# A DLRM tower on one Trainium2 core: first chunk tile by tile, a sum over d in four pieces, late columns' passes ahead of layer 1's last sum

## What is computed

```python
e  = stack([tbl_f[ids[:, f]] for f in range(39)], axis=1)        # 512 x 39 x 16 (b, field, d)
z0 = einsum('bid,bjd->bdij', e, e)                               # all pairs, per d
cur0 = relu(einsum('bdk,kl->bld', z0.reshape(b, d, 39*39), W0))  # 128 features
next_h, direct0 = split(cur0, 2, axis=1)                         # 64 + 64
z1 = einsum('bid,bjd->bdij', e, next_h)
cur1 = relu(einsum('bdk,kl->bld', z1.reshape(b, d, 39*64), W1))  # 128 features
z  = sum(concatenate([direct0, cur1], axis=1), axis=-1)          # the sum over d: 512 x 192
h  = relu(concatenate([z, dense_ctx], axis=1) @ W_top1 + b_top1) # 512 x 512
y  = relu(h @ W_top2 + b_top2) @ W_top3                          # 512 x 1
```

## Time and profile before

| | us |
|---|---|
| median of three runs | 447.23 |
| the three runs | 426.04, 447.23, 447.35 |
| the profiled execution | 425.06 |
| its span, first to last instruction | 423.2 |
| PE / DVE / POOL / ACT busy in the span | 393.7 / 347.0 / 284.4 / 226.8 |

### The profile page before, as it was taken

How to read it: one execution, slowest core, us unless ns; L and a number is a source line. 1 busy time by engine, 2 the same in 40 slices (tenths; PEclk the granted TensorE clock), 3 DMA queues, 4 the chain that set the end, 5 groups by cost and what they waited for, 6 DMA issues and landing times.

```text
span 423.2 us, 4060 instructions
## 1 busy us (share of the span) xinstructions
PE 393.7 (93%) x1417; PEld 248.8 (59%) x1417; DVE 347.0 (82%) x198; ACT 226.8 (54%) x225; POOL 284.4 (67%) x164
## 2 busy tenths in 40 slices
PE   0695999999899979999899999999999999999997
PEld 0452656565666646564665656566656565666655
DVE  1205879979999799897989999999999999999930
ACT  1333466474656466473648475665747474655422
POOL 5777878989888889898888888888888600000000
PEclk9899899999999989999899999999999999999999
DMA  7194969596978979694978969797969395997000
GB/s 285 29 207 98 284 170 222 167 227 152 268 172 217 209 191 219 172 266 107 251 180 217 232 203 233 192 250 191 265 171 284 108 283 184 269 259 199 1 2 0
DMA packets 27862, 80.80 MB, mean 191 GB/s; under 512 B 7265, under 2 KB 16225, under 8 KB 20034
## 3 DMA queue, kind: packets, MB, share of 16 engines
q1 hardware_dynamic: 22354, 78.43, 71.0%
q0 software_dynamic: 5120, 1.32, 2.9%
q10 hardware_dynamic: 368, 0.80, 0.5%
HBM read 76.58 MB, written 3.93 MB: 190 GB/s over the span
## 4 chain that ended last, share of the span: by engine, by line
PE 51%; POOL 36%; issue 7%; DMA 5%; ACT 0%; DVE 0%; SPq 0%
POOL found L285 36%; PE acc L517 10%; PE acc L543 8%; PE acc L544 8%; PE acc L551 8%; PE acc L562 6%; PE sums L500 4%; DMA found<-in_table_dram,rows_sb 3%; PE acc L558 2%; PE spread L591 2%; DMA x_parts<-x_rows 1%; PE spread L530 1%; DMA x_rows<-found 1%; PE sums L580 0%; PE sums L582 0%
## 5 line engine op out<-in xcount | busy, mean ns | idle before, releaser
L285 POOL DMA_INDIRECT found<-in_table_dram,rows_sb x160 | 284.2, 1776 | 51.2 <-issue 48.5
L428 DVE TENSOR_TENSOR z_lo<-z,z_hi 128x2048 fp32r<-128x2048 f32 x64 | 146.1, 2284 | 8.6 <-ACT z_hi L328 8.4
L328 ACT ACTIVATE z_hi<-z 128x2048 fp32r<-128x2048 f32 x63 | 120.4, 1912 | 57.7 <-DVE z L420 57.7
L420 DVE TENSOR_TENSOR z<-x_wide,h 128x2048 f32<-128x2048 f32 x64 | 145.4, 2285 | 6.8 <-DMA x_wide<-x_rows 6.4
L543 PE MATMUL acc<-z_hi,w_hi 128*128 128x512 f32 x256 | 108.8, 425 | 0.0
L517 PE MATMUL acc<-squares,w 128*128 128x512 f32 (+1 forms) x224 | 108.0, 599 | 0.0
L544 PE MATMUL acc<-z_hi,w_lo 128*128 128x512 f32 x256 | 102.3, 399 | 0.0
L304 ACT ACTIVATE squares<-sums 128x1024 f32<-128x1024 f32 x64 | 58.5, 913 | 61.3 <-PE sums L500 61.3
L551 PE MATMUL acc<-z_lo,w_hi 128*128 128x512 f32 x256 | 82.2, 443 | 0.0
L551 PEld LDWEIGHTS acc<-z_lo,w_hi 128*128 128x128 f32 x256 | 48.2, 188 | 23.1 <-issue 15.4
L543 PEld LDWEIGHTS acc<-z_hi,w_hi 128*128 128x128 f32 x256 | 49.5, 193 | 14.8 <-issue 4.2
(11 more groups left out here) (49 smaller groups left out, 135.0 us busy)
## 6 DMA issues: line engine op xcount, KB each, us to landing
x_wide<-x_rows SPq DMA_DIRECT2D x64, 512.0 KB, 7.6
x_wide<-x_rows SPq DMA_DIRECT2D x112, 256.0 KB, 9.5
x_parts<-x_rows SPq DMA_DIRECT2D x31, 128.0 KB, 2.5
x_rows<-found SPq DMA_DIRECT2D x16, 240.0 KB, 2.6
x_wide<-x_rows SPq DMA_DIRECT2D x16, 192.0 KB, 7.2
found<-in_table_dram,rows_sb POOLq DMA_INDIRECT x160, 7.0
w_sb<-in_w_dram SPq DMA_DIRECT2D x1, 1280.0 KB, 8.4
x_wide<-x_rows SPq DMA_DIRECT2D x16, 64.0 KB, 6.7
```

Source lines behind the costliest of these rows:

```text
L285: pool.indirect_dma_start(out=found[:, b, 2, s * D:s * D + D], out_offset=None, in_=table, in_offset=bass.IndirectOffsetOnAxis(ap=rows_sb[ ...
L328: nc.scalar.activation(z_hi[:, n % RING], z[:, n % RING], ACT.Copy).then_inc(hi_done, 1)
L420: nc.vector.tensor_tensor(z[:, n % RING], x, h[:, c % 2, :].unsqueeze(1).to_broadcast([P, QUADS, N]), ALU.mult).then_inc(multiplied, 1)
L428: nc.vector.tensor_tensor(z_lo[:, n % RING], z[:, n % RING], z_hi[:, n % RING], ALU.subtract).then_inc(lo_done, 1)
```

## The change

- Chunk 0's layer 0 goes by single tiles (`add_up_tile`, `square_tile`, `contract0_tile`) with semaphores counted in tiles; later chunks keep groups of two.
- At the start DVE does `split(0)` ahead of the addition of W0's halves; PE does 17 dummy products at once and 9 behind the small `mix` product, and no longer waits for the first split.
- PE does `contract1_hi(0)` ahead of chunk 1's first `add_up`, and `contract1_lo(0)` ahead of the second.
- ACT's `split(2)` stands at n = 0 in place of g = 1; DVE's `reduce0(1)` stands at n = 4 in place of n = 6.
- `reduce1` is four instructions of 8 samples each in place of one of 32.
- After the last `contract1_lo`, PE does the products of `feat_b` for the late columns at once, then half of `y_of(early)`, and after `reduce1` only the products of `feat_a`; the other half of `y_of(early)` stands behind them.

```diff
+def tiles0(q):
+    return q // ND * T0 + q % ND * 2
@@ SP, and likewise evict0 and hid1_of
-                    sp.wait_ge(summed, ND * (c - BUFS + 1))
+                    sp.wait_ge(summed, T0 * (c - BUFS + 1))
@@ ACT
+            def square_tile(t):
+                rows = slice(0, P) if t < T0 - 1 else slice(HALF, P)
+                act.wait_ge(summed, t + 1)
+                if t >= 2 * RING0:
+                    act.wait_ge(contracted0, t - 2 * RING0 + 1)
+                nc.scalar.activation(squares[rows, t // 2 % RING0, t % 2, :], sums[rows, t % 2, :],
+                                     ACT.Square).then_inc(squared, 1)
...
-            for d in range(ND):
-                square(d)
+            for t in range(T0):
+                square_tile(t)
             split(1)
             evict0(0)
...
                     if g < 2 and c + 1 < CHUNKS:
                         square(ND * (c + 1) + 2 + g)
+                    if n == 0:
+                        split(2)
...
-                    if g == 1 and c + 2 < CHUNKS:
+                    if g == 1 and 0 < c < CHUNKS - 2:
                         split(c + 2)
@@ DVE
             def reduce1(c):
                 dve.wait_ge(evicted1, c + 1)
-                nc.vector.tensor_reduce(feat_a[:, c * CB:c * CB + CB],
-                                        cur1[:, :].rearrange("p (b d) -> p b d", d=D), AX.X,
-                                        ALU.add).then_inc(reduced1, 1)
+                for i in range(0, CB, CB // 4):
+                    last = nc.vector.tensor_reduce(feat_a[:, c * CB + i:c * CB + i + CB // 4],
+                                                   cur1[:, i * D:(i + CB // 4) * D].rearrange("p (b d) -> p b d", d=D),
+                                                   AX.X, ALU.add)
+                last.then_inc(reduced1, 1)
...
+            split(0)
             dve.wait_ge(w0_in, 32)
...
-            split(0)
             dve.wait_ge(w1_hi_ready, 1)
...
+                    if n == G - 1:
+                        reduce0(1)
                     if is_v(n):
                         low_part(n)
...
-                    if n == G + 1:
-                        reduce0(1)
@@ PE
+            def add_up_tile(t):
+                if t == 0:
+                    pe.wait_ge(placed[0], 32)
+                if t >= 2:
+                    pe.wait_ge(squared, t - 1)
+                nc.tensor.matmul(sums[:, t % 2, :], select_sb[:, t, :], x_parts[:, 0, :],
+                                 start=True, stop=True).then_inc(summed, 1)
...
+                if batch == late:
+                    return
                 nc.tensor.matmul(hid1_acc[m][:, batch], wt1a_sb[:, cols], feat_a[:, batch],
                                  start=False, stop=True).then_inc(hid1_done, 1)
+
+            def hid1_end(m):
+                nc.tensor.matmul(hid1_acc[m][:, late], wt1a_sb[:, m * P:m * P + P], feat_a[:, late],
                                  start=False, stop=True).then_inc(hid1_done, 1)
...
             pe.wait_ge(select_ready, 1)
+            keep_busy(acc0, 17)
             pe.wait_ge(w0_ready, 1)
...
-            pe.wait_ge(found_hi_done, 1)
-            keep_busy(acc0, 21)
-            add_up(0)
+            keep_busy(acc0, 9)
+            add_up_tile(0)
+            add_up_tile(1)
             spread_out(0)
             pe.wait_ge(w0_ready, 2)
-            for d in range(ND):
-                if d + 1 < ND:
-                    add_up(d + 1)
-                contract0(d)
+            for t in range(T0):
+                if t + 2 < T0:
+                    add_up_tile(t + 2)
+                contract0_tile(t)
             keep_busy(acc1, 14)
...
+            contract1_hi(0)
             add_up(ND)
-            contract1_hi(0)
+            contract1_lo(0)
             add_up(ND + 1)
             contract0(ND)
-            contract1_lo(0)
...
             contract1_lo(G * CHUNKS - 1)
-            y_of(early)
             pe.wait_ge(reduced0, CHUNKS)
+            pe.wait_ge(hid1_relu, M1 // P)
+            for m in range(M1 // P):
+                hid1_of(m, late)
+            y_of(0, early)
             pe.wait_ge(reduced1, CHUNKS)
             for m in range(M1 // P):
-                hid1_of(m, late)
+                hid1_end(m)
+            y_of(1, early)
```

More of the change, by code:

```diff
@@ L501, in add_up, with contract0_tile @@
                                             start=True, stop=True)
-                last.then_inc(summed, 1)
+                last.then_inc(summed, len(DUOS[q % ND]))
+            def add_up_tile(t):
[5 more added lines that the diff above has]
+                                 start=True, stop=True).then_inc(summed, 1)
+            def contract0_tile(t):
+                pe.wait_ge(squared, t + 1)
+                rows = slice(0, P) if t < T0 - 1 else slice(HALF, P)
+                nc.tensor.matmul(acc0[:, :], w0[rows, t, :], squares[rows, t // 2 % RING0, t % 2, :],
+                                 start=(t == 0), stop=(t == T0 - 1)).then_inc(contracted0, 1)
             def keep_busy(acc, count):
@@ L518, in contract0 @@
                                             start=(t == 0), stop=(t == T0 - 1))
-                last.then_inc(contracted0, 1)
+                last.then_inc(contracted0, len(DUOS[d]))
             def spread_out(n):
@@ L593, in hid2_of, with y_of @@
                 last.then_inc(hid2_done, 1)
-            def y_of(batch):
-                for k in range(M2 // P):
-                    pe.wait_ge(hid2_relu, k + 1 + (M2 // P if batch == late else 0))
-                    last = nc.tensor.matmul(y_acc[:, batch], wt3_sb[:, k:k + 1], hid2[k][:, batch],
-                                            start=(k == 0), stop=(k == M2 // P - 1))
-                last.then_inc(y_done, 1)
+            def y_of(k, batch):
+                pe.wait_ge(hid2_relu, k + 1 + (M2 // P if batch == late else 0))
+                last = nc.tensor.matmul(y_acc[:, batch], wt3_sb[:, k:k + 1], hid2[k][:, batch],
+                                        start=(k == 0), stop=(k == M2 // P - 1))
+                if k == M2 // P - 1:
+                    last.then_inc(y_done, 1)
             pe.wait_ge(select_ready, 1)
+            keep_busy(acc0, 17)
             pe.wait_ge(w0_ready, 1)
@@ L670, in _ @@
             contract1_lo(G * CHUNKS - 1)
-            y_of(early)
             pe.wait_ge(reduced0, CHUNKS)
+            pe.wait_ge(hid1_relu, M1 // P)
+            for m in range(M1 // P):
+                hid1_of(m, late)
+            y_of(0, early)
             pe.wait_ge(reduced1, CHUNKS)
             for m in range(M1 // P):
-                hid1_of(m, late)
+                hid1_end(m)
+            y_of(1, early)
             for m in range(M2 // P):
                 hid2_of(m, late)
-            y_of(late)
+            for k in range(M2 // P):
+                y_of(k, late)
 def layout(inputs):
```

18 lines of the change are left out of this document (8 added, 10 removed).

## The result

The changed kernel took 445.5 us in the median of 14 executions (442.39 to 459.37). The kernel before took 446.8 beside it, also over 14 (426.04 to 450.22). The comparison on record, 1.050 [1.041, 1.059], calls the changed kernel 5% slower, but it leaves out every execution over 1.5% above its kernel's fastest, and by that rule the single one at 426.04 stands for the kernel before. Over all 14 executions each, the medians differ by -0.3%. So the change gained nothing of the 33 us that were forecast. Of the kernel before 1 of 14 was under 430 us, of the changed one none; 14 executions can't tell that from chance, for the kernel before, run 57 times in all, has 4 such. The profile ahead of the prediction, of an execution of 425.06, is of this rare kind.

What follows compares the result with a forecast made beforehand. TensorE's 22.26 us a chunk sets the pace, with starved GpSimd gathers delaying it. 425.06 - 10.2 (starvation) - 2.0 (TensorE's startup order) - 0.2 (tail) = 412.7, plus 0.8 for late `x_parts`: 413.5 us, range 409 to 430.

Steps and rivals of the forecast that it cites:

- The pace, and the 10.2 us lost in chunks 0 to 7: Chunk loop: TensorE needs 22.26 us a chunk; the first seven periods lose 10.2 us to late `x_parts` and lowered clock.
- W: DVE's open stretch once a chunk (`reduce0`, `reduce1`, multiplication out of PSUM), which holds up no gather: 3.31 us, forecast 3.5 (3.8).
- The reading of the 447-us executions: Slower executions were read as ones where gather starvation lasted longer; their further 22 us would go with it.
- five starved chunks more are the 21 us: Chunk loop: a starved chunk loses 4 us or so, so five more explain 447 against 426.
- Held up for one instruction, and let in: `reduce1` in four: the third gather start falls 0.12 us behind W's end, waits one DVE instruction; nearly all 10.2 us go.
- +0.5, then it falls ahead of the end and is free, both ends are safe: `reduce1` in four, upper cost bound: W of 3.8 us puts the third gather start ahead of W's end, unheld.
- TensorE's order at the start, -2.0: Startup: `contract1_hi(0)` moves into the wait for `x_parts`, 1.8 to 3.4 us off, some 1.3 back; bounds -3 and -0.5.
- `split(2)` earlier, 0 or +1: Startup, ACT's order: no gain since PE is not waiting; +1 us if chunk 2's gathers land late and `square` waits.
- DVE at the start, 0 under a cover of 2.4: Startup, DVE and tiles: +1.9 us of moved work, less waits by tile, both covered by 2.4; up to +3 at half clock.
- The tail, -0.2: After the last reduce: +0.2 to +0.5 for pieces, -0.9 for early `feat_b` products, about 0.75 back; bounds -0.5 and +0.5.
- D: Rival: starvation lasts in most runs for a cause other than W; 445 us, chance 0.12.
- E: Rival: dear pieces put the fourth gather start on the bad place, each chunk starves twice; 468 us, chance 0.05.

Runs made afterwards that it cites:

- run 57: Not a run's label: the kernel before, unchanged, was run 57 times in all; median 445.5 us, 4 of them under 430, 46 over 440.
- before_again: The kernel before, unchanged, run again for a trace of a usual execution: median 446.8 us, profiled 446.74.
- before_four: The kernel before with only `reduce1` in four instructions: median 443.9 us (417.2 to 448.3).
- before_hold: The kernel before, with GpSimd starting chunk 2's gathers only when the first h is evicted: median 422.4 us (416.9 to 439.6).
- before_tail: The kernel before with only the tail's new order behind the last `contract1_lo`: median 444.7 us, profiled 418.22.
- hold_eight: The kernel before with chunk 2's gathers held until the first h, and `reduce1` in eight pieces: median 459.5 us, profiled 465.42.
- after_one: The changed kernel with `reduce1` as one instruction again: median 437.2 us, profiled 421.21.
- after_hold: The changed kernel with GpSimd's chunk 2 gathers held until the first h: median 442.8 us, profiled 429.34.
- before_plain: The kernel before with only chunk 0 gathered, later chunks' rows by plain SyncE transfer (output not the reference's): median 410.4 us.
- after_plain: The changed kernel with only chunk 0 gathered, later chunks' rows by plain SyncE transfer (output not the reference's): median 410.1 us.
- after_nodummy: The changed kernel without its 17, 9 and 14 dummy products: median 434.1 us, profiled 452.32.
- hold_apart: The kernel before with chunk 2's gathers held until the first h, and `reduce1` moved from g = 4 to g = 2: median 422.8 us.
- hold_four: The kernel before with chunk 2's gathers held until the first h, and `reduce1` in four pieces: median 424.0 us.
- before_hold2: The kernel before with chunk 2's gathers held until the first h, repeated on another chip: median 432.4 us (418.1 to 452.0).

## Why the prediction was wrong

**The pace, and the 10.2 us lost in chunks 0 to 7: right.** The undisturbed period is 22.26 in every kernel, with W of any length.

**The reading of the 447-us executions: wrong, and the largest error.** The step "five starved chunks more are the 21 us" was marked as not shown by a trace. `before_again` shows it false: +30.9 us at the first product, -9.2 afterwards, with 0.7 us lost to starvation; `before_four`, 448.33 in its profile, has 89.3 and 0.1. The sum was made on an execution that only 4 of 57 come near, and the other 22 us were booked to the same cause and then taken off. Of the error against the profiled execution, 453.8 - 413.5 = 40.3 us, the start carries 85.1 - 54.3 = 30.8. I should have kept the two apart: a profile of the good kind can't say what the bad kind is made of. The sum would then have read 413.5 for the rare kind and 413.5 + 22, about 435, for the usual one.

**"Held up for one instruction, and let in": wrong.** This is the step on `reduce1` in four. Its terms were right: W of 3.5 (measured 3.47), a start 0.12 behind (0.13), 0.18 us of DVE time. The map from place to fate was wrong. It rested on one gather that passed at 0.24; a neighbouring place on a scale with both outcomes (0.36 in, 0.38 not) was no bound. And DVE had waited 0.88 just before that gather, while all three starved ones of the earlier trace rows came behind a W without a wait, which is the condition that the runs show. In the changed kernel four of five starts at 0.13 or 0.14 starved, in all kernels with four pieces 9 of 14, so the 10.2 us stayed: 9.1. They lasted up to 18.6 us, against 11.6 in the profile ahead of the prediction, but not by the pieces: with `reduce1` whole there are gathers of 14.0 and 18.4 us, too (`before_hold`, `before_tail`). The bound "+0.5, then it falls ahead of the end and is free, both ends are safe" was wrong too; `hold_eight`, with W at 3.72 for the forecast's 3.8, is nearly this case and lost 42 us. The rule of the Trainium skill, page SBUF — State Buffer (Who interferes with whom), is half confirmed again: gathers are held by DVE's instructions with two SBUF inputs and pass beside `tensor_reduce`. A second party is held there for the current instruction; here it was eight in a row (18.61 us). The page VectorE: DVE Perf Modes of the Trainium skill (section on the TRN2 errata) warned of small pieces for their fixed latency. The trace agrees with its size (0.87 against 0.69 for three more instructions). The harm came another way.

**TensorE's order at the start, -2.0: sign right, and lost.** The first product came at 51.9 in `after_one`, 4.4 us earlier than before, and 0.8 earlier with plain loads. In no profile with gathers did chunk 1's product come earlier than 79.0.

**`split(2)` earlier, 0 or +1: mis-sized.** The prediction saw that `square` would wait if chunk 2's rows came late, and priced that at 1 us. In `after_one` and `after_hold` ScalarE stood 8.65 and 8.84 us there, TensorE 5.12 and 5.30, and chunk 1's product came 31.3 and 32.6 us behind chunk 0's instead of 22.7. In `after_one` that took back more than the 4.4 us won before; `after_hold` has the hold besides. Without gathers the two profiles of the same order take 0.4 and 0.0 us more than `before_plain` for that period.

**DVE at the start, 0 under a cover of 2.4: not the cause.** `after_plain` has all these edits and its first product at 50.2. In the changed kernel the moved copy L475 waits 9.83 us, but for a late increment.

**The tail, -0.2: measured +0.2.** From the last eviction to the end: 8.12 before, 8.30 after. The two moves of the tail are the +0.18, as `before_tail` has it without the pieces. The term took 0.9 off for the products of `feat_b`; but the halves of `y_of(early)` now stand ahead of and behind the products of `feat_a`, and in `before_tail` `hid2_of` starts 2.14 us behind the end of the last reduce, before 2.00.

**The rivals.** D gave 445 for "starvation lasts for a cause other than W", and 445.5 came. The number fits by luck, the mechanism doesn't: it isn't starvation. E's picture (starts on a bad place chunk by chunk, 468) came true to a few us in `hold_eight`, with 465.4, but by pieces at their forecast price, in another kernel; that number, too, is luck.

**What stays open.** Why TensorE's increments reach their readers up to 27 us late in most executions (46 of 57 took over 440 us) and little or not at all in the rare good one. Shown is that it doesn't come without gathers behind chunk 0 (none in three profiles, and 14 executions of three kernels are all under 414 us) and that holding them shortens it. The last late one comes 1.1 to 5.4 us behind the end of the first series of gathers in five profiles with a late start, and 2.5 to 3.3 us behind it in four of the kernels with a hold; in `after_nodummy` it comes at 66.97, within a second series that ends at 69.83. This is order in time and no proof of a cause: a late TensorE also keeps the buffers full and so stops the gathers. Not shown is what carries the delay. Open is also what decides, behind an unbroken W, whether a gather starves (46 of 56 did).

## The best version seen

`before_hold` beats both kernels: medians of 422.4 and 432.4 where the kernel before had 446.1 and 448.1 beside it on the same chips. `hold_apart` gave 422.8 (before: 448.1). In the four kernels with this hold and W up to 3.5, 12 of 17 executions were under 430, against 4 of 57. They are not steady: single ones still reach 452 and 457. `before_plain` says that 410 is there for a kernel whose rows come without these gathers; it leaves out the gathering itself.

## What to carry to other kernels

Where executions scatter by 5%, profile one of each kind before costing anything, and book no term of the sum on the kind that you haven't seen. The starts of one instruction per chunk tell at once whether time goes at the start or in the loop. And a cure that moves an event by 0.2 us within a pattern whose safe places are known from single cases is a gamble; compare cases in the same place first, for what they have in common can be something else (here a DVE that ran without a break). Take the contention away rather than tune around it: 410 us with plain loads is what that is worth here at most.

## What the hardware showed unexpectedly

- Instructions waiting for TensorE went on 8 to 27 us after its matmuls had ended, at the start of a kernel, with gathers in flight. TensorE then idles, and its granted clock falls. Length, busy of PE, PEld, DVE, ACT, POOL, clock, DMA share, GB/s in the changed kernel:

```profile
30.00:40.00 10.00, 0.00 (x0) 0.00 (x0) 0.99 (x1) 0.00 (x0) 7.87 (x8) 0.50 0.27 48
...
50.00:60.00 10.00, 2.41 (x4) 0.84 (x3) 0.00 (x0) 1.19 (x3) 3.36 (x4) 0.67 0.05 4
```

- 0.50 is 1.2 GHz, the lower level; TensorE did nothing in those ten microseconds. With plain loads every stretch of ten from 20 to 90 us is at 1.00.
- A gather was held for 18.61 us through eight DVE instructions. Every starved one went on 0.81 to 0.83 us behind the end of such an instruction, nearly always at DVE's first break.
- Eight or sixteen small reductions in place of one, 0.4 to 0.9 us of DVE time, raised the median by 35 and 28 us on top of kernels with the same hold on the same chip (`hold_four`, `before_hold2`).
